# A two-layer attention kernel: feed-forward output in two turns instead of four, a new table of steps, and the first bodies' loads on two queues

## The reference, cut to what matters

```python
xn = _layernorm(x)
x = x + _L0_attn_ref(xn, ...) + _L0_ffn_ref(xn, ...)     # layer 0
xn = _layernorm(x)
x = x + _L1_attn_ref(xn, ...) + _L1_ffn_ref(xn, ...)     # layer 1
```

## Time and profile before

| what | value |
|---|---|
| median of 3 runs | 1753.87 us (1744.63 to 1756.75) |
| the profiled execution | 1737.72 us, its span 1735.9 us |
| busy, share of the span | PE 87%, DVE 80%, ACT 76%, POOL 55% |
| start, until body 0's first score tile | 108.4 us |
| layer 0 alone, bodies 1 to 13 | 574 us for 13 bodies, 42.0 to 49.0 us each |
| both layers | from 728 to 882 us |
| layer 1 alone | 15 bodies of about 57 us, and the tail |

### The profile page before, as it was taken

How to read it: one execution, slowest core, us unless ns; L and a number is a source line. 1 busy time by engine, 2 the same in 40 slices (tenths; PEclk the granted TensorE clock), 3 DMA queues, 4 the chain that set the end, 5 groups by cost and what they waited for, 6 DMA issues and landing times.

```text
span 1735.9 us, 33268 instructions
## 1 busy us (share of the span) xinstructions
PE 1517.9 (87%) x11850; PEld 625.8 (36%) x11850; DVE 1387.9 (80%) x2459; ACT 1313.5 (76%) x2614; POOL 950.9 (55%) x1176
## 2 busy tenths in 40 slices
PE   4788888888888888888899998999999999999995
PEld 2454444344444444443233323233233322332331
DVE  2378888788888888888888888888888888888881
ACT  2247887677787777776787888888888888888884
POOL 2124665555565555554555655566456546565555
PEclk9789999899999999999899999999999999999998
DMA  8322223222333223232332222222331223222200
GB/s 282 61 51 74 75 76 66 76 75 69 76 72 82 76 61 75 70 82 64 59 62 55 51 55 64 59 49 55 68 63 51 42 70 63 52 58 47 65 14 19
DMA packets 133125, 116.41 MB, mean 67 GB/s; under 512 B 16856, under 2 KB 125664, under 8 KB 132960
## 3 DMA queue, kind: packets, MB, share of 16 engines
q1 hardware_dynamic: 126272, 100.64, 25.2%
q0 software_dynamic: 4096, 8.40, 1.5%
q10 hardware_dynamic: 2592, 5.24, 0.9%
HBM read 79.63 MB, written 33.55 MB: 65 GB/s over the span
## 4 chain that ended last, share of the span: by engine, by line
PE 48%; DVE 22%; ACT 11%; DMA 6%; POOL 5%; issue 5%; SPq 2%; POOLq 0%; DVEq 0%; ACTq 0%
PE pv_acc L636 15%; PE scores_transposed L652 11%; ACT probs L958 5%; PE scores_transposed L790 4%; DVE maxs L1194 3%; DMA stacks<-parts_scratch 3%; PE scores_for_max L673 3%; DVE maxs L1163 3%; DMA stacks<-mT 2%; DVE maxs L1185 2%; PE scores_for_max L798 2%; DVE maxs L1190 2%; ACT xn L859 2%; PE scores_transposed L762 2%; PE scores_for_max L702 2%
## 5 line engine op out<-in xcount | busy, mean ns | idle before, releaser
L958 ACT ACTIVATE probs<-scores_transposed 128x512 f32<-128x512 f32 x1664 | 907.9, 600 | 189.8 <-PE scores_transposed L652 177.1
L652 PE MATMUL scores_transposed<-stacks 62*128 62x512 bf16 (+3 forms) x2048 | 574.7, 346 | 67.3 <-ACT probs L958 38.6
L1333 POOL TENSOR_TENSOR probs<-probs,near_bias 128x512 f32<-128x512 f32 x256 | 325.4, 1271 | 354.2 <-ACT probs L958 351.7
L636 PE MATMUL pv_acc<-probs,vals 128*32 128x512 f32 (+3 forms) x4096 | 478.6, 540 | 13.2 <-POOL probs L1307 11.4
L1163 DVE TENSOR_REDUCE maxs<-scores_for_max 128x2 f32<-128x1024 f32 x340 | 411.6, 1222 | 87.0 <-PE scores_for_max L673 84.3
L652 PEld LDWEIGHTS scores_transposed<-stacks 62*128 62x128 bf16 x2048 | 150.7, 94 | 600.6 <-ACT probs L958 294.6
L673 PE MATMUL scores_for_max<-stacks 60*128 60x512 bf16 x1024 | 329.0, 387 | 10.8 <-DVE maxs L1163 5.9
L677 PE MATMUL scores_for_max<-stacks 60*128 60x512 bf16 (+3 forms) x1024 | 250.0, 309 | 8.7 <-DMA stacks<-parts_scratch 7.3
L1194 DVE TENSOR_REDUCE maxs<-scores_for_max 128x1 f32<-128x512 f32 x256 | 175.1, 684 | 100.2 <-PE scores_for_max L689 89.8
L1166 DVE TENSOR_REDUCE maxs<-scores_for_max 128x1 f32<-128x512 f32 x344 | 226.5, 685 | 24.3 <-PE scores_for_max L673 21.8
L1307 POOL TENSOR_SCALAR_AFFINE_SELECT probs<-probs 128x512 f32<-128x512 f32 x256 | 174.1, 693 | 121.8 <-ACT probs L958 121.6
(11 more groups left out here) (130 smaller groups left out, 1988.5 us busy)
## 6 DMA issues: line engine op xcount, KB each, us to landing
stacks<-parts_scratch SPq DMA_DIRECT2D x768, 64.0 KB
parts_scratch<-parts SPq DMA_DIRECT2D x64, 384.0 KB, 2.6
x_tile<-in_L_attn_x_dram SPq DMA_DIRECT2D x16, 256.0 KB, 2.9
probs<-in_fc_B_dram ACTq DMA_DIRECT2D x1, 4096.0 KB, 19.3
stage_a<-in_fc_A_T_dram SPq DMA_DIRECT2D x1, 4096.0 KB, 16.9
stacks<-mT SPq DMA_DIRECT2D x256, 4.0 KB
x_res<-in_L_attn_x_dram SPq DMA_DIRECT2D x16, 256.0 KB, 3.2
x_tile<-x_between_layers SPq DMA_DIRECT2D x16, 256.0 KB, 2.8
```

Source lines behind the costliest of these rows:

```text
L636: last = mm(acc[VW * j:VW * j + VW, q0:T], columns[:, first:first + VW], probs[:, row, column:column + width], start=(kt == 0 and pu % PAI ...
L652: last = mm(st[:, bank, column:column + T - q0], ks[p][rows, h, P * kt:P * kt + P], qs[p][rows, h, q0:T], start=True, stop=True)
L958: fn(probs[:, row, :], st[:, B.use(("st", u, number)).bank, :], ACT.Exp, scale=SCALE).then_inc(s["exp_done"], 1)
L1333: g.tensor_tensor(diag, diag, near_bias[:, kt, :].unsqueeze(1).broadcast_to([P, G, P]), ALU.mult).then_inc(s["emul_pool"], 1)
```

## The change

- **Layer 1's Y.** Y0 to Y3 become Y0 (slot 57) and Y1 (slot 61). Each makes two token tiles with the same matmuls side by side in one bank, and ACT copies 128x256 numbers in one instruction.
- **Table of steps.** In layer 0, MIX now stands ahead of LN, NORM goes from slot 7 to 11, XT from 14 to 19, PJ0 from 29 to 24, QT from 47 to 50, KT from 59 to 57. In layer 1, VP goes from 33 to 31, QT from 42 to 34, MT2 from 35 to 40; other steps move by one slot.
- **Setup loads.** Ten of the 18 setup loads go from SP to ACT, where they stand ahead of the factors of W1.
- **First stacks.** For body 0, the 12 key transfers are issued by ACT after its first body, beside SP's 12 of the queries. The buffer they land in is cleared earlier by POOL, the other buffers later.
- **Compose.** `COMPOSE_FROM` is 32, and W2's first twelve products stand two to a slot.

```diff
-COMPOSE_FROM = 24
+COMPOSE_FROM = 32
+COMPOSE_SECOND = [min(slot + min(slot, 6), NF * NC) for slot in range(NG * NT * G + 1)]
...
-        "OA": (19, 0, -1), "XT": (21, 0, 2), "AT": (25, 0, -1), "H3": (28, 0, 1), "PR": (30, 0, -1),
-        "VP": (33, 0, 1), "MT2": (35, 0, 0), "QT": (42, 1, 2), "KT": (44, 2, 2), "OB": (48, 0, 0),
-        "Y0": (53, 0, 1), "Y1": (57, 0, 1), "MT3": (59, 0, 1), "Y2": (61, 0, 1), "Y3": (62, 0, 1)},
+        "OA": (19, 0, -1), "XT": (21, 0, 2), "AT": (25, 0, -1), "H3": (28, 0, 1), "PR": (30, 0, -1),
+        "VP": (31, 0, 1), "QT": (34, 1, 2), "MT2": (40, 0, 0), "KT": (44, 2, 2), "OB": (48, 0, 0),
+        "Y0": (57, 0, 1), "Y1": (61, 0, 1), "MT3": (59, 0, 1)},
...
-    0: {"LN": (0, 2), "MIX": (2, 1), "NORM": (7, 2), "VALUES": (19, 1), "POST": (21, -1),
+    0: {"MIX": (1, 1), "LN": (3, 2), "NORM": (11, 2), "VALUES": (15, 1), "POST": (21, -1),
...
+        def load_stack_rows(eng, s, side, p):
+            for t, part in enumerate((Q_PARTS, K_PARTS)[side]):
+                heads = parts_dram[side, part].rearrange("(h e d) n -> e d h n", e=E, d=HD)
+                for e in range(E):
+                    row = HALF * e + HD * t
+                    eng.dma_start((qs, ks)[side][p][row:row + HD, :, :], heads[e]).then_inc(s["stack_loaded"], 16)
...
-                        for side in ((0, 1), ())[u] if both else (u,):
+                        sides = (0,) if layer == 0 and B.number == FIRST + 1 else (0, 1)
+                        for side in (sides, ())[u] if both else (u,):
                             load_stack(side)
...
+                for n in range(*COMPOSE_SECOND[slot:slot + 2]):
+                    f, c = n // NC, n % NC
...
+                                for t in range(2 * n, 2 * n + 2):
+                                    for f in range(NF):
+                                        last = mm(work[:, D * (t % 2):D * (t % 2) + D], big[:, f, P * t:P * t + P],
+                                                  w2[:, f, :], start=(f == 0), stop=(f == NF - 1))
...
+            for dst, src in loads:
+                act.dma_start(dst, src).then_inc(setup_in, 16)
             load_for_compose(act, 0)
             load_for_compose(act, 1)
...
-                                fn(ffn[:, B.parity(1), t, :], work[:, 0:D], ACT.Copy).then_inc(taken, 1)
+                                fn(ffn[:, B.parity(1), 2 * n:2 * n + 2, :].rearrange("p t d -> p (t d)"),
+                                   work[:, 0:2 * D], ACT.Copy).then_inc(taken, 1)
...
             act.wait_ge(setup_pool, 5)
+            act.wait_ge(S[0]["parts_stored"], 32)
+            load_stack_rows(act, S[0], 1, 0)
...
+            g.memset(stacks[:, :, 0, :].bitcast(F32), 0.0).then_inc(setup_pool, 1)
 
             def clear_first_buffers():
+                pool.wait_ge(setup_dve, 5)
                 g.memset(vals[:, 0], 0.0).then_inc(setup_pool, 1)
-                g.memset(stacks[:, :, 0, :].bitcast(F32), 0.0).then_inc(setup_pool, 1)
```

69 lines of the change are left out of this document (31 added, 38 removed), and 8 rows, old and new, of the table WORK_USES.

## The result

The changed kernel takes 1736.85 us (median of 20 runs, 1720.42 to 1753.08), beside 1746.85 (20 runs) for the kernel before on the same chip: ratio 0.9948, interval 0.9922 to 0.9973. A gain of 10 us, where 40 were forecast: the time lies near the upper end of the range, and the forecast of 1714 is 23 us too low. Of the 17 us between the 1753.87 from which the forecast started and this time, 7 are the kernel before's own median, which came out lower over 20 runs; that the time lies inside the range of 1683 to 1743 is luck, for 0.9948 of 1753.87 would be 1744.7. The profiled execution is the slowest of the 20 (1753.08), so its stages are read one by one and against a second trace of the kernel before.

A forecast was written before the change was run, and what follows sets the result against it. No engine was held full: layer 0 lost time to PE's waits and half clock, the start to transfers and PE; layer 1's second half was PE's work. Start 13, layer 0 22, layer 1 5: 40 us, 1753.87 to 1714; range 1683 to 1743.

The forecast's parts named there:

- The 4 MB for W1: Start: W1's factors, issued 5.4 us later, land at about 26.4 us after 19.3; KT ends at 41.0 instead of 47.8.
- The stack loads: Start: body 0's 24 loads over two queues land between 59.3 and 68.8 us; the maxima start 6.8 to 11.6 earlier.
- If PE no longer idles, the 14.5 us at the half clock shrink by up to 5: Start: the 1.2 GHz stretch after the maxima begin gets up to 5 us shorter, within a start gain of 13.
- MIX ahead of LN takes ten small DVE instructions from before `fa`: Layer 0: with this order PE's FR step no longer waits for `fa` on DVE, 0.8 us a body.
- NORM behind FK's result lets POOL mask sooner: Layer 0: moving NORM later on ACT lets POOL start its masks earlier; no size of its own given.
- QT three slots later removes its wait: Layer 0: QT at slot 50 no longer waits for SCALE_QK on DVE, 1.2 us a body.
- The half of 2.95 us: Layer 0: half of 0.8 + 1.2 + 0.95 (half clock) was taken, 1.55 a body, 22 us over 14 bodies.
- only the start gains: Rival, chance 0.19: layer 0's waits go but reappear at the next thing DVE is late for; 1740 us.
- The rival of the shared engines: Start, chance 0.12: stack loads on two queues share the same DMA engines; the start gains 9 us, not 13; 1718.
- QT was to use the 1.0 us in which PE idles in the second half: Layer 1: QT's 1.12 us, moved to slot 34, fills PE's idle time; 0.3 us a body taken, 5 in all.
- The gain case: Rival, chance 0.22: both queues add, the half clock leaves both layers, layer 1 gives 0.6 a body; 71 us, so 1683.
- The slower rival, crowded steps: Layer 1, chance 0.07: PR, VP and QT within five slots starve DVE; 3.5 us a body lost, 56 in all, 1775.

The follow-up runs named there:

- l0_only: The kernel before with only the changed table of steps of layer 0; 1746.61 us, ratio 1.0047.
- best_mix: best with one more edit, layer 0's MIX at slot 1 ahead of LN at slot 3, NORM still at 7; 1742.16 us, ratio 1.0009.
- best: The kernel before with W1's products behind KT, layer 0's QT at 50 and KT at 57, and layer 1's changed table and Y; 1696.33 us, ratio 0.9733.
- again: The changed kernel, unaltered, run once more for a second trace; 1737.54 us, ratio 0.9932 to the kernel before.
- warm: The changed kernel plus nine products without use on PE ahead of its wait for the stack loads; 1734.48 us, ratio 0.9860 to the kernel before.
- before: The kernel before, unaltered, first trace, from which the forecast was made; 1753.87 us.
- before2: The kernel before, unaltered, run again for a second trace; 1741.03 us, ratio 1.0011.
- l1_only: The kernel before with only the changed table of layer 1 and its Y in two turns; 1726.40 us, ratio 0.9962.

## Why the prediction was wrong

**Start, forecast -13, measured 0.** Three terms failed. *The 4 MB for W1*: the forecast took the 19.3 us of before for a transfer that is now issued later; it took 22.9, and KT ended at 45.4 instead of 41.0. *The stack loads*: two queues were left a chance of adding rate; they gave none. Above all, "If PE no longer idles, the 14.5 us at the half clock shrink by up to 5": that price was read from one execution. In a second one of the same program the stretch lasted over 44 us. PE did go on idling (8.92 us), and with the changed start it never had the short stretch in seven traces. So the largest lever of the start was there, 18 us of clock behind PE's wait, but the change didn't pull it.

**Layer 0, forecast -22, measured +5 and +17 in the profile, against the two traces of the kernel before, and +0.5% of the time by itself (l0_only).** The step "MIX ahead of LN takes ten small DVE instructions from before `fa`: FR's wait, 9.9 / 12 = 0.8 us, should go" failed: the wait went and 2.8 us a body came (best_mix against best), the clock's part among them. The text costed the ten LN instructions by who waited behind them, and not by who waits for them: POOL's `rstd` and ACT's NORM, with the exponentials behind. "NORM behind FK's result lets POOL mask sooner" failed too: from 200 to 640 us `pv`'s wait for POOL is 23.9 us, where it was 6.2, and a part of it is really the wait for the copy to `accS`. "QT three slots later removes its wait" held, but of the 1.2 us a body 0.4 were left at the full clock, as FR waited longer: with KT's move and the clock it is 0.7% of the time. (The half of 2.95 us that the forecast took is 1.48 and not 1.55, 1 us over the stage.) The rival "only the start gains", in which the waits of layer 0 turn up elsewhere, had layer 0 right and the start wrong; its 1740 is 3 us from the result by an opposite path, which is luck. The rival of the shared engines was right on the loads.

**Layer 1, forecast -5, measured -8 in the profile and -12 against the second trace.** The sign held, and that Y by itself gives nothing. The reason failed: QT was to use the 1.0 us in which PE idles in the second half, but that idle time stayed, and at the full clock a body is no shorter (56.1 us against 55.95). What the runs show in its place is the clock, 1.00 instead of 0.98 to 0.99, a term that was not in the 0.3 us. The gain case had it: the half clock gone from layer 1 and 0.6 us a body. The slower rival, crowded steps, didn't come: the wait of the score tiles for DVE's maxima grew from 5.5 to 9.5 us over 14 bodies, far from its price; with Y alone it is already 9.3.

**What stays open.** The three parts alone give 1.0032, 1.0047 and 0.9962, a product of 1.004, while the change has 0.9948 and 0.9932 (again); each interval is near 0.004 wide to a side, and all of them together allow for some 0.007, so the parts don't quite add up. Whether the edits act on one another isn't shown. Why the stretch at 1.2 GHz behind PE's wait lasts some 15 us in one execution and over 44 in another of the same program isn't settled either. In warm a wait of 1.07 us was followed by it, in best one of 1.13 was not; what the five traces without it share is that PE made W1 and W2 right ahead of the maxima. That this is the cause is argued, not shown. In best, FR still waits 1.3 us a body.

## What to carry to other kernels

Before a step is moved ahead of another on one engine, follow the one that falls behind through all engines that wait for it: ten instructions of a few tenths of a microsecond cost 46 us through two other queues and the clock. A clock stretch or the end of a chain of loads can be a property of an execution: with one and the same start the stack loads were in at 75.6, 76.4, 77.3 and 85.0 us (before, l0_only, before2, l1_only). Take a second trace before a term of a sum rests on it. Read bodies by their granted clock before a gain is put down to a step: layer 1 gained 8 to 12 us, and at the full clock its bodies are as long as before. Work that PE has to do anyway belongs where it would wait for a chain of transfers (W1 and W2 behind KT gave 15 to 18 us at the start; nine products without use in the same wait gave nothing), and a table that gains as a whole should be split in halves, as each may hide the other.
